# Ternary weights in a fused graph-and-feed-forward kernel: the lower comparison becomes a Sign on ScalarE

## The reference, cut to what matters

```python
def _quant_weight(w):
    s = jnp.clip(jnp.mean(jnp.abs(w)), EPS, None)
    wq = jnp.clip(jnp.round(w / s), -1.0, 1.0) * s
    return w + jax.lax.stop_gradient(wq - w)

def _bitlinear(x, w):
    return jnp.einsum('bsi,oi->bso', _quant_act(x), _quant_weight(w))

x = x + _L1_gnn_ref(_layernorm(x, axis=-1), edge_index, L1_gnn_W, L1_gnn_b)
h = jax.nn.gelu(_bitlinear(x, w1), approximate=False)     # w1: 4096 x 1024
return _bitlinear(h, w2)                                   # w2: 1024 x 4096
```

## Time and profile before

| | us |
|---|---|
| median of three runs | 1343.07 |
| lowest and highest of them | 1341.3, 1346.01 |
| the profiled execution, time | 1343.57 |
| the profiled execution, span of the trace | 1341.8 |
| TensorE busy in the span | 1116.6 |
| VectorE busy | 797.8 |
| ScalarE busy | 481.2 |

### The profile page before, as it was taken

How to read it: one execution, slowest core, us unless ns; L and a number is a source line. 1 busy time by engine, 2 the same in 40 slices (tenths; PEclk the granted TensorE clock), 3 DMA queues, 4 the chain that set the end, 5 groups by cost and what they waited for, 6 DMA issues and landing times.

```text
span 1341.8 us, 20170 instructions
## 1 busy us (share of the span) xinstructions
PE 1116.6 (83%) x7645; PEld 633.8 (47%) x7645; DVE 797.8 (59%) x1086; ACT 481.2 (36%) x550; POOL 161.6 (12%) x209
## 2 busy tenths in 40 slices
PE   0577769996289999996539998898898999999998
PEld 0566644444255556663514444444443444444444
DVE  8766566767635555551466756888865544445531
ACT  2256644535244444440412222334313333333331
POOL 6000022331110000000042100212110000000000
PEclk9877779997589999999559999999999999999999
DMA  1525424426356666642431205666600000000000
GB/s 56 204 102 186 153 65 153 172 114 252 136 148 232 225 231 219 233 183 91 155 94 63 94 1 173 202 215 194 205 16 0 17 17 16 16 16 16 16 16 28
DMA packets 51036, 158.50 MB, mean 118 GB/s; under 512 B 12218, under 2 KB 12540, under 8 KB 46880
## 3 DMA queue, kind: packets, MB, share of 16 engines
q1 hardware_dynamic: 41663, 136.10, 28.7%
q0 software_dynamic: 9312, 21.58, 5.2%
HBM read 137.00 MB, written 20.65 MB: 117 GB/s over the span
## 4 chain that ended last, share of the span: by engine, by line
PE 61%; DVE 19%; issue 7%; ACT 5%; DMA 5%; POOL 1%; DVEq 1%; ACTq 0%; SPq 0%
PE ps L1001 11%; PE ps L1026 10%; PE ps L920 9%; PE ps L904 8%; PE ps L835 5%; PE ps L983 4%; DVE fq L1830 4%; DVE stats L1393 2%; PE ps L745 2%; DVE xn L1534 2%; DMA fnat_a<-in_L_ffn_w 2%; DVE x L1765 1%; PE ps L969 1%; PE ps L764 1%; PE ps L891 1%
## 5 line engine op out<-in xcount | busy, mean ns | idle before, releaser
L1001 PE MATMUL ps<-w1q,xqt 128*128 128x512 fp8e4 x640 | 141.0, 381 | 13.1 <-ACT xqt L1282 13.1
L1026 PE MATMUL ps<-w2q,hqt 128*128 128x512 fp8e4 x640 | 143.0, 379 | 8.7 <-ACT hqt L1291 8.7
L1865 DVE TENSOR_REDUCE hm<-hf 128x1 f32<-128x512 f32 x80 | 54.3, 685 | 94.8 <-ACT hf L1286 94.8
L1001 PEld LDWEIGHTS ps<-w1q,xqt 128*128 128x128 f16 x640 | 62.2, 98 | 88.7 <-issue 16.2
L1026 PEld LDWEIGHTS ps<-w2q,hqt 128*128 128x128 f16 x640 | 61.1, 98 | 78.6 <-issue 10.2
L1286 ACT ACTIVATE hf<-ps,fs 128x512 f32<-128x512 f32 x80 | 55.0, 688 | 90.9 <-PE ps L1001 90.9
L904 PE MATMUL ps<-xdh,w1h 128*128 128x314 f16 x256 | 77.1, 301 | 0.8 <-DVE xdl L1693 0.8
L904 PE MATMUL ps<-xdh,w1l 128*128 128x314 f16 x256 | 76.5, 299 | 0.0
L904 PE MATMUL ps<-xdl,w1h 128*128 128x314 f16 x256 | 76.4, 299 | 0.0
L612 POOL TENSOR_TENSOR rtmp<-mv,consts 128x1 f32<-128x1 f32 x40 | 12.7, 319 | 508.6 <-DVE mv L1398 508.5
L920 PE MATMUL ps<-w2h,hth 128*128 128x512 f16 (+1 forms) x192 | 73.0, 380 | 0.0
(11 more groups left out here) (274 smaller groups left out, 2290.7 us busy)
## 6 DMA issues: line engine op xcount, KB each, us to landing
abs_in<-in_L_ffn_w SPq DMA_DIRECT2D x32, 1024.0 KB, 4.8
wstage<-in_L_ffn_w SPq DMA_DIRECT2D x32, 1024.0 KB, 12.3
fnat_a<-in_L_ffn_w SPq DMA_DIRECT2D x48, 512.0 KB, 4.3
eo_d<-eo SPq DMA_DIRECT2D x16, 512.0 KB
bias_b<-in_L_ffn_w SPq DMA_DIRECT2D x16, 512.0 KB, 4.1
xs_d<-xs_all SPq DMA_DIRECT2D x10, 512.0 KB, 4.4
out_x<-out_t SPq DMA_DIRECT2D x9, 512.0 KB, 2.7
b2b<-in_L_ffn_b SPq DMA_DIRECT2D x8, 512.0 KB, 8.8
```

The lines of the kernel that those rows point to most:

```text
L1001: last = mm(ps[:, n % 4, :], xqt[:, u, k, :], w1q[:, k, n * 512:(n + 1) * 512], start=(k == 0), stop=(k == KD - 1))
L1026: last = mm(ps[:, 4 + h, :], hqt[:, k, :], w2q[:, k, h * 512:(h + 1) * 512], start=(k == 0), stop=(k == KF - 1))
L1865: last = v.tensor_reduce(hm[:, u, n:n + 1], hf[:, u, n * 512:(n + 1) * 512], AX.X, ALU.max, apply_absolute_value=True)
```

## The change

The first of the two comparisons is taken from VectorE. ScalarE instead computes `fsgn`, the sign of the weight plus the threshold, which is -1 or 1 (the threshold is the activation's bias, read from `sw[:, 4:6]`, one value for each partition). VectorE's remaining instruction compares the weight with the threshold, which gives 1 or 0, and takes the minimum of that and `fsgn`. The table of minus half of the mean is gone. `upper_sign(n + 1)` stands ahead of the copy of piece `n` in ScalarE's program, and waits for the fetched piece and for the ternary piece `n - 1`.

```diff
-        fneg = sb("misc", "fneg", [P, 2, D], F8)
+        fsgn = sb("misc", "fsgn", [P, 2, D], F8)
...
             act.wait_ge(s_hsl, 1 + NT)
+            def upper_sign(n):
+
+                act.wait_ge(s_fn[n % 4], 16 * (n // 4) + 16)
+                if n >= 2:
+                    act.wait_ge(s_fq, 4 + n - 1)
+                cp(fsgn[:, n % 2, :], fnat[n % 4], ACT.Sign, bias=sw[:, 4 + n // 32:5 + n // 32],
+                   saturate=False).then_inc(s_fsgn, 1)
+
+            act.wait_ge(s_swh, 1)
+            upper_sign(0)
             for n in range(64):
+                if n < 63:
+                    upper_sign(n + 1)
                 act.wait_ge(s_ft, 2 + n + 1)
...
-            steps.inc(v.tensor_scalar(sw[:, 4:6], sw[:, 2:4], 0.5, None, ALU.mult))
-            do(v.tensor_scalar(sw[:, 6:8], sw[:, 2:4], -0.5, None, ALU.mult))
+            v.tensor_scalar(sw[:, 4:6], sw[:, 2:4], 0.5, None, ALU.mult).then_inc(s_swh, 1)
...
-            def below(n):
-
-                if n >= 2:
-                    dve.wait_ge(s_fq, 4 + n - 1)
-                dve.wait_ge(s_fn[n % 4], 16 * (n // 4) + 16)
+            def weight_piece(n):
+
                 m = n // 32
-                v.tensor_scalar(fneg[:, n % 2, :], fnat[n % 4], sw[:, 6 + m:7 + m], None, ALU.is_lt,
-                                saturate=False).then_inc(s_fneg, 1)
-
-            def weight_piece(n):
-
-                m = n // 32
-                if n < 63:
-                    below(n + 1)
-                dve.wait_ge(s_fneg, n + 1)
+                dve.wait_ge(s_fsgn, n + 1)
                 dve.wait_ge(s_ft, n + 1)
                 v.scalar_tensor_tensor(out=fq[:, n % 2, :], in0=fnat[n % 4], scalar=sw[:, 4 + m:5 + m],
-                                       in1=fneg[:, n % 2, :], op0=ALU.is_gt, op1=ALU.subtract).then_inc(s_fq, 1)
-
-            below(0)
+                                       in1=fsgn[:, n % 2, :], op0=ALU.is_gt, op1=ALU.min).then_inc(s_fq, 1)
+
             for i in range(8):
                 for k in range(8):
                     weight_piece(8 * i + k)
```

More of the change, by code:

```diff
@@ L381, in build_kernel @@
         s_swm = sem("s_swm")
+        s_swh = sem("s_swh")
         s_fn = [sem(f"s_fn{i}") for i in range(4)]
-        s_fneg = sem("s_fneg")
+        s_fsgn = sem("s_fsgn")
         s_fq = sem("s_fq")
```

## The result

The changed kernel takes 1356.95 us (median of four runs, 1355.37 to 1359.83) against 1343.11 us before (four runs, 1341.3 to 1346.01). The ratio is 1.0103, with an interval of 1.0079 to 1.0128: the change makes the kernel some 14 us slower. The profiled execution took 1359.83 us with a span of 1358.1 us.

The account below looks back on a forecast made before the run. VectorE was taken as the bound, TensorE close behind. With the sign in a loop, 19.42 + 6 x 21.84 + 16.63 = 167.1 us against 158.3, 8.8 more, gave 1352.4 from 1343.57; range 1347 to 1359.4.

Parts of the forecast that it names:

- The bound before: In the stage before the change, VectorE sets the pace at 1.98 us a piece, TensorE close behind at 1.74.
- The loop: Transposes, ScalarE's copy, sign, VectorE's `fq`, back to TensorE: 4.08 us over two pieces, 2.04 us a piece.
- The loss: After the stage, all work is ordered behind TensorE, so the 8.8 us more pass on in full.
- The sign: ScalarE's new instruction, 128 x 1024, taken as 1.15 us; near bounds 1.01 and some 1.26, far bound 0.753.
- Transfers: Weight fetches into four buffers: nearly all earlier waits disappear, already in the sum; far bound 7 us more.
- The clock: Rival: TensorE's clock falls after idling ahead of each step's fourth piece, up to 12 us, 1364 us; chance 5 in 100.
- a clock below 1.00 in the steps: Sign against the forecast: TensorE's granted clock was to be 1.00 from 824 us on.
- the stretch: From the first to the last piece's transposes in the stage: 167.1 us forecast against 158.3, 8.8 us more.
- The idle time ahead of the fourth piece: TensorE's wait before each step's fourth transposes: 2.65 us forecast, against 1.73 us before.
- a case without and a case with a fall: TensorE idling 1.73 us in steps, clock 1.00, and 3.94 us ahead of the stage, clock 0.64; 2.65 lies between.
- The range: Whole kernel: 1347 to 1359.4 us, the top including up to 7 us for late transfers; forecast's chance 82 in 100.
- the overlap: ScalarE's copy and sign overlapping: if lost, 24 x 0.11 = 2.7 us more, 1355.1 us.

Follow-up runs that it names:

- The order experiment: Changed kernel with ScalarE's sign of piece n+2 ahead of the copy of piece n; 1325.89 us against 1341.66 for the kernel before, ratio 0.9879.
- the half sign: Changed kernel with the sign taken over only 512 of 1024 columns, the rest filled once with zeros; 1343.03 us, ratio 1.0009 to the kernel before.
- the fill: Changed kernel with ten more TensorE products in the idle time ahead of the fourth piece, waits in unchanged order; 1352.38 us, ratio 1.0076 to the kernel before.

## Why the prediction was right, and where it was short

**The bound before** (VectorE at 1.98 us a piece, TensorE close behind at 1.74) holds: relieved of the comparison, with the sign ahead of the copy and `agg` behind the second piece, the stage falls to TensorE's pace, 17.39 us a step. With both comparisons kept and `agg` at that place, VectorE is busy 141.39 of 154.84 us and the stage stays near 19.5.

**The loop** through copy and sign was the step on which everything rested, and it held: 4.08 us forecast and 4.09 read, 2.74 us to the third `fq` forecast and read, 21.84 and 21.86 us for a step. The order experiment shows it as cause, and the half sign shows that the sign is three times on the path of a step (1.28 us for three times 0.43). The loss passes on in full, as forecast: from the last transposes to the end it takes 359.5 us before and 359.9 after.

**The sign** was taken as 1.15 us from `hs_h`; it took 1.138 to 1.148 (medians of 1.139 and 1.145 for its two kinds of buffer). The estimate of 1.133 us from the Trainium skill ("ScalarE: Activation LUTs", What ACT_TABLE_LOAD costs) is as near. The difference is worth at most 0.4 us of the sum, and no measurement here could tell it.

**Transfers** were counted as hidden, and were: steps of equal clock agree to 0.01 us, where before they spread from 20.25 to 21.39.

**The clock** is the term that was mis-sized. The prediction put a fall at 5 in 100, as a rival in place of the forecast, with up to 12 us, and at nothing in the sum; and it named a clock below 1.00 in the steps as a sign that it was wrong. That sign came: four falls in the stretch in each of two profiles, at 1.06 to 1.27 us each, together 4.45 and 4.7 us, on top of the forecast. The idle time ahead of the fourth piece was nearly right: 2.65 us from start times, 2.47 read. To take it as lying between a case without and a case with a fall was fair, but the half sign has 2.47 us too and no fall, so its length alone would not have decided it. With the idle time filled, the stretch is 167.20 us, which is the forecast.

**The range** held in part by luck. The measured 1356.95 us lie above the 1355.1 us that the sign and the overlap could reach. They are inside only by the 7 us set aside for late transfers, and no late transfer was seen in the steps; the clock used that room. The forecast's 1352.4 us against the fill's 1352.38 says little either, as the kernel before ran at slightly different times in the two groups; the stretch is the better comparison.

**The rest of the first profile's difference** to that of before lies outside the stretch: 1.3 us ahead of the stage (TensorE's first product of it at 818.89 instead of 817.60 us), and 1.2 us in it before the first transposes, where the clock came up later than before. In the second profile of the changed kernel the first product came at 816.30 and the clock did not fall there, so neither is put down to the change.

## What to carry to other kernels

Before work goes to an idle engine, see whether the new instruction would stand behind one that waits for the end of the same loop. Here that place alone decided between 14 us slower and 16 us faster. Count the hand-overs of the loop in program order, not the busy time. A block that follows a wait (here `agg`) should be put ahead of it when its own inputs are long there. When a step leaves TensorE idle longer than before, price the clock as a possible addition to the forecast and not as an alternative to it.

## What was not expected of the hardware

An idle time of 2.35 to 2.47 us on TensorE, once in a step of some 22 us, came with a fall of the granted clock right behind it in four steps of seven, in three profiles of two kernels. With that idle time filled, in two profiles, there was none. But the kernel with half of the sign had the same 2.47 us in all seven steps, in steps of 20.58 us, and no fall either; the kernel before had none with 1.73 us, though its longest step had 3.14 us of idling in all (21.39 less 18.25), more than that one's 2.50. So neither the longest idle time nor the sum of a step decides it alone, and what does stays open. In one and the same kernel the fall came in different steps (the second, fourth, sixth and seventh in one profile; the fourth, fifth, seventh and eighth in the other).

Even the 3.94 us of idling ahead of the stage was not always followed by slow products: it was in the first profiles of both kernels, and not in the second of the changed one nor in that of the kernel with the sign ahead of the copy. And the order of two waits ahead of an instruction had a price: with the one that comes last in time put last, each loop was 0.09 us longer.
